# Mixture-of-experts stage: units of two tiles in place of single tiles, with gathered rows transposed first

## The reference, cut to what matters

```python
def reference(x, ...):                      # x: (2, 2048, 256) fp32
    xn = layernorm(x)
    # attention part: a scan over time whose weights depend on time_decay and time_first alone
    k, v = xn @ key_w.T, xn @ value_w.T
    r = sigmoid(xn @ recep_w.T)
    att = (r * wkv_scan(time_decay, time_first, k, v)) @ out_w.T
    # per step: p=max(pp,tf+pp); e1=exp(pp-p); e2=exp(tf+pp-p); wkv=(e1*aa+e2*v)/(e1*bb+e2+1e-6)
    #           p2=max(pp,td+pp); aa=exp(pp-p2)*aa+exp(td+pp-p2)*v; bb=exp(pp-p2)*bb+exp(td+pp-p2)
    # mixture of 8 experts, two per token, and one shared expert
    scores = softmax(xn @ gate_w.T + gate_b); top_w, top_i = top_k(scores, 2)
    y = sum over the two experts e of top_w * ((silu(xn@w1e.T+b1e) * (xn@w3e.T+b3e)) @ w2e.T + b2e)
    z = (silu(xn@ws1.T+bs1) * (xn@ws3.T+bs3)) @ ws2.T + bs2
    return x + att + y + z
```

## Time and profile before

| | |
|---|---|
| median of three runs | 540.8 us (540.36 to 542.17) |
| the profiled execution, its run | 540.79 us |
| its span | 539.1 us |
| mean granted clock of TensorE | 0.946 |
| PE busy | 471.3 us, 87% |
| PEld busy | 381.2 us, 71% |
| DVE busy | 428.3 us, 79% |
| ACT busy | 239.9 us, 44% |
| POOL busy | 260.9 us, 48% |

### The profile page before, as it was taken

How to read it: one execution, slowest core, us unless ns; L and a number is a source line. 1 busy time by engine, 2 the same in 40 slices (tenths; PEclk the granted TensorE clock), 3 DMA queues, 4 the chain that set the end, 5 groups by cost and what they waited for, 6 DMA issues and landing times. The chain is left out here.

```text
span 539.1 us, 10721 instructions
## 1 busy us (share of the span) xinstructions
PE 471.3 (87%) x2624; PEld 381.2 (71%) x2625; DVE 428.3 (79%) x963; ACT 239.9 (44%) x543; POOL 260.9 (48%) x311
## 2 busy tenths in 40 slices
PE   1885094999899999999999868899999999999997
PEld 1332042787788878777877757687889888888887
DVE  7797993578878888888888835998978888797964
ACT  1677251366556656565655555314232324242321
POOL 2000003535656666666566546787656573747200
PEclk9998555899989999999999997999999999999999
DMA  7999201383333334333433327527171625254011
GB/s 246 387 362 319 96 0 29 107 276 113 125 101 113 107 116 127 108 118 115 125 109 108 109 76 230 189 89 233 43 212 57 198 82 171 84 170 131 26 39 41
DMA packets 58553, 73.95 MB, mean 137 GB/s; under 512 B 6848, under 2 KB 47552, under 8 KB 58528
## 3 DMA queue, kind: packets, MB, share of 16 engines
q1 hardware_dynamic: 52048, 55.94, 31.0%
q0 software_dynamic: 6480, 17.70, 12.2%
HBM read 45.39 MB, written 28.18 MB: 136 GB/s over the span
## 5 line engine op out<-in xcount | busy, mean ns | idle before, releaser
L834 POOL DMA_INDIRECT xg<-xn_rows,picked x71 | 71.2, 1003 | 56.0 <-POOL picked L831 38.7
L1319 POOL DMA_INDIRECT yg<-expert_rows,rows x64 | 71.4, 1115 | 23.6 <-issue 17.1
L898 PE MATMUL ps_g<-w_hi,x_hi 128*128 x142 | 57.5, 405 | 0.8 <-issue 0.8
L898 PE MATMUL ps_g<-w_lo,x_hi 128*128 x142 | 56.9, 401 | 0.0
L898 PE MATMUL ps_g<-w_hi,x_lo 128*128 x142 | 56.9, 401 | 0.0
L831 POOL COPY picked<-tile_tok 128x1 int32 (+1 forms) x71 | 14.3, 201 | 86.5 <-POOLq L317 82.5
L1350 PE MATMUL ps_w<-col_hi,s_hi 128*128 128x512 f32 x128 | 51.0, 399 | 1.6 <-DVE res L1545 1.0
L971 ACT ACTIVATE act<-ps_g 128x256 f32<-128x256 f32 x71 | 27.2, 383 | 52.0 <-PE ps_g L901 48.4
L1351 PE MATMUL ps_w<-col_lo,s_hi 128*128 128x512 f32 x128 | 50.2, 392 | 0.0
L1352 PE MATMUL ps_w<-col_hi,s_lo 128*128 128x512 f32 x128 | 50.2, 392 | 0.0
L1452 ACT ACTIVATE sact<-ps_w,vec_b 128x512 f32<-128x512 f32 x32 | 22.0, 687 | 59.6 <-PE ps_w L1352 47.6
(11 more groups left out here) (192 smaller groups left out, 1412.2 us busy)
## 6 DMA issues: line engine op xcount, KB each, us to landing
expert_rows<-y SPq DMA_DIRECT2D x71, 128.0 KB
table<-mix_tables SPq DMA_DIRECT2D x16, 384.0 KB, 5.2
xin<-x SPq DMA_DIRECT2D x16, 256.0 KB, 4.2
xn_rows<-xn SPq DMA_DIRECT2D x16, 256.0 KB, 4.7
xn_columns<-xT SPq DMA_DIRECT2D x8, 512.0 KB, 4.5
col<-xn_columns SPq DMA_DIRECT2D x8, 512.0 KB, 7.3
mix_tables<-coef SPq DMA_DIRECT2D x16, 256.0 KB
res<-x SPq DMA_DIRECT2D x16, 256.0 KB
```

The costliest lines, as they stand in the source:

```text
L834: pool.indirect_dma_start(out=xg[a.buf(NG)][:], out_offset=None, in_=xn_d[:, :], in_offset=bass.IndirectOffsetOnAxis(ap=picked[a.buf(NG)][ ...
L898: nc.tensor.matmul(out, x[:, k, :], w[:, ds(e, 1), k, cols].rearrange("p o n -> p (o n)"), start=(k == 0 and n == 0), stop=False)
L1319: pool.indirect_dma_start(out=yg[a.buf(2)][:, k, q, :], out_offset=None, in_=y_d[:, :], in_offset=bass.IndirectOffsetOnAxis(ap=picked[a.bu ...
```

## The change

The expert stage works in units of two tiles (DUOS = 36, the last one with a single tile), and all its loops are written out. Each operation of ScalarE and VectorE on a tile becomes one on two tiles (128x512 in place of 128x256), each store one of 256 KB. A gather copies two columns of indices at once and issues two indirect DMAs, each with a semaphore step ahead; `xg` has four buffers of two tiles, and TensorE waits for both. `ps_x`, `ps_h`, `act1` and `hid` have one buffer of two tiles in place of two of one tile. TensorE's order for unit a is: read the two expert numbers of unit a+2, turn_x(a+3), turn_h(a), down(a-1), up(a+2). So the gathered rows are transposed first and the gated rows second. VectorE's order is gate(a+1), hidden(a+1), cut_h(a), cut_x(a+3), with hidden directly behind gate.

The table task works in pieces of 256 time steps (PIECE = 256, 8 pieces), a piece per four units, that is eight tiles. Its buffers are shared: `dif` lies in raw_vr, one of the two `firsts` in col0, the halves are written to `firsts` and `decay` themselves, the reciprocal overwrites `den`, and coef overwrites `firsts`. The loads of raw_vr and col0 move to the end of the stage. The first piece's growth, sums and halves stand ahead of the first tile's x_hi and x_lo. In the mix a table is one transfer.

```diff
-ROUNDS = -(-TILES // 4)
-REST = TILES - 4 * (ROUNDS - 1)
+DUOS = -(-TILES // 2)
-PIECE = 128
+PIECE = 256
...
-        picked = [sb(f"picked{b}", [P, 1], I32) for b in range(NG)]
-        xg = [sb(f"xg{b}", [P, C], F32) for b in range(NG)]
-        x_hi = [sb(f"x_hi{b}", [P, KC, P], F32R) for b in range(2)]
-        x_lo = [sb(f"x_lo{b}", [P, KC, P], F32R) for b in range(2)]
-        act1 = [sb(f"act1{b}", [P, FF], F32) for b in range(2)]
-        hid = [sb(f"hid{b}", [P, FF], F32) for b in range(2)]
-        h_hi = [sb(f"h_hi{b}", [P, KC, P], F32R) for b in range(2)]
-        h_lo = [sb(f"h_lo{b}", [P, KC, P], F32R) for b in range(2)]
+        picked = [sb(f"picked{b}", [P, 2], I32) for b in range(NG)]
+        xg = [sb(f"xg{b}", [P, 2, C], F32) for b in range(NG)]
+        x_hi = [sb(f"x_hi{b}", [P, 2, KC, P], F32R) for b in range(2)]
+        x_lo = [sb(f"x_lo{b}", [P, 2, KC, P], F32R) for b in range(2)]
+        act1 = sb("act1", [P, 2, FF], F32)
+        hid = sb("hid", [P, 2, FF], F32)
+        h_hi = [sb(f"h_hi{b}", [P, 2, KC, P], F32R) for b in range(2)]
+        h_lo = [sb(f"h_lo{b}", [P, 2, KC, P], F32R) for b in range(2)]
...
-        rden = sb("rden", [P, KC, PIECE], F32)
-        coef = sb("coef", [P, 2, KC, PIECE], F32)
-        ps_x = [bank(f"ps_x{b}", [P, KC, P]) for b in range(2)]
-        ps_g = [bank(f"ps_g{b}", [P, 2 * FF]) for b in range(2)]
-        ps_h = [bank(f"ps_h{b}", [P, KC, P]) for b in range(2)]
-        ps_y = [bank(f"ps_y{b}", [P, C]) for b in range(2)]
+        ps_x = bank("ps_x", [P, 2, KC, P])
+        ps_g = [bank(f"ps_g{b}", [P, 2, 2 * FF]) for b in range(2)]
+        ps_h = bank("ps_h", [P, 2, KC, P])
+        ps_y = [bank(f"ps_y{b}", [P, 2, C]) for b in range(2)]
...
+                def store_decay(v):
+                    sp.wait_ge(t_exp, v + 1)
+                    sp.dma_start(tab_d[v:v + 1, :, 0:1].rearrange("o p n k t -> p (o n k t)"),
+                                 decay[:].rearrange("p k t -> p (k t)")).then_inc(t_est, 16)
+
+                def store_coef(v):
+                    sp.wait_ge(t_coef, v + 1)
+                    sp.dma_start(tab_d[v:v + 1, :, 1:3].rearrange("o p n k t -> p (o n k t)"),
+                                 firsts[v % 2].rearrange("p n k t -> p (n k t)")).then_inc(t_cst, 16)
+
+                for a in range(DUOS + 1):
+                    if a > 0:
+                        store(a - 1)
+                    v, r = divmod(a, 4)
+                    if r == 1 and v < NPIECE:
+                        store_decay(v)
+                    if r == 2 and 0 < v <= NPIECE:
+                        store_coef(v - 1)
+                    if 0 < a <= len(loads):
+                        sp.dma_start(*loads[a - 1]).then_inc(c_ld, 16)
+                    if a == 4 * LAST_V + 1:
+                        sp.wait_ge(t_sides, NPIECE)
+                        sp.dma_start(raw_vr[:], wvr).then_inc(c_vr, 16)
+                    if a == 4 * LAST_V + 3:
+                        assert (LAST_V - 1) % 2 == 0
+                        sp.wait_ge(t_cst, LAST_V * 16)
+                        sp.dma_start(col0[:].rearrange("p k n -> p (k n)"), columns).then_inc(c_col, 16)
...
                 def gather(a):
+                    b, n = a % NG, tiles(a)
+                    at_least(pool, c_tx, a - NG + 1)
+                    nc.gpsimd.tensor_copy(picked[b][:, 0:n], tile_tok[:, 2 * a:2 * a + n]).then_inc(c_idx, 1)
+                    pool.wait_ge(c_idx, a + 1)
+                    for t in range(n):
+                        pool.sem_inc(c_go, 1)
+                        pool.indirect_dma_start(
+                            out=xg[b][:, t, :], out_offset=None, in_=xn_d[:, :],
+                            in_offset=bass.IndirectOffsetOnAxis(ap=picked[b][:, t:t + 1], axis=0)
+                        ).then_inc(c_gath[b], 16)
+
+                def denominator(v):
+                    own = OwnIn(pool, t_pool, At(0, v, NPIECE), 2)
+                    f = firsts[v % 2]
+                    pool.wait_ge(t_bb, v + 1)
+                    pool.wait_ge(t_exp_f, v + 1)
+                    at_least(pool, t_coef, v)
+                    own.link(nc.gpsimd.tensor_tensor(den[:], f[:, 0], s_b[:, :, 0:PIECE], ALU.mult))
+                    own.link(nc.gpsimd.tensor_tensor(den[:], den[:], f[:, 1], ALU.add))
                     own.close()
                     nc.gpsimd.tensor_scalar(den[:], den[:], 1e-6, 2.0, ALU.add, ALU.mult).then_inc(t_den, 1)
 
+                def factors(v):
+                    f = firsts[v % 2]
+                    pool.wait_ge(t_rec, v + 1)
+                    nc.gpsimd.tensor_tensor(f, f, den[:, None].broadcast_to([P, 2, KC, PIECE]),
                                             ALU.mult).then_inc(t_coef, 1)
 
+                for a in range(NG):
+                    gather(a)
+                for a in range(DUOS):
+                    v, r = divmod(a, 4)
+                    if a + NG < DUOS:
+                        gather(a + NG)
+                    if r == 1 and 0 < v <= NPIECE:
+                        factors(v - 1)
+                    if r == 2 and v < NPIECE:
+                        denominator(v)
+                for n, (raw, hi, lo) in enumerate((vr, col)):
                     pool.wait_ge(c_whi, n + 1)
                     nc.gpsimd.tensor_tensor(lo[:], raw[:], hi[:].bitcast(F32), ALU.subtract).then_inc(c_wlo, 1)
 
             @block.tensor
             def _(pe):
+                def experts(a):
+                    _, values = nc.values_load_multi_w_load_instructions(
+                        tile_exp[0:1, 2 * a:2 * a + tiles(a)], engines=[mybir.EngineType.PE],
+                        min_val=0, max_val=E - 1)
+                    return values
+
                 def turn_x(a):
+                    pe.wait_ge(c_gath[a % NG], a // NG * 32 + tiles(a) * 16)
+                    at_least(pe, c_xlo, a)
+                    for t in range(tiles(a)):
+                        for k in range(KC):
+                            mm = nc.tensor.transpose(ps_x[:, t, k, :], xg[a % NG][:, t, k * P:(k + 1) * P], ident[:])
                     mm.then_inc(c_tx, 1)
...
+                def down(a, es):
+                    pe.wait_ge(c_hlo, a + 1)
+                    at_least(pe, c_yc, a - 1)
+                    for t in range(tiles(a)):
+                        mm = three(ps_y[a % 2][:, t, :], h_hi[a % 2][:, t], h_lo[a % 2][:, t], es[t],
+                                   slice(2 * FF, WALL))
+                    mm.then_inc(c_y, 1)
+
+                es = {}
+                turn_x(0)
+                turn_x(1)
+                es[0] = experts(0)
+                up(0, es[0])
+                turn_x(2)
+                es[1] = experts(1)
+                up(1, es[1])
+                for a in range(DUOS):
+                    if a + 2 < DUOS:
+                        es[a + 2] = experts(a + 2)
+                    if a + 3 < DUOS:
+                        turn_x(a + 3)
+                    turn_h(a)
+                    if a > 0:
+                        down(a - 1, es.pop(a - 1))
+                    if a + 2 < DUOS:
+                        up(a + 2, es[a + 2])
+                down(DUOS - 1, es.pop(DUOS - 1))
...
+                def halves(v):
+                    f = firsts[v % 2]
+                    act.wait_ge(t_dif, v + 1)
+                    at_least(act, t_cst, (v - 1) * 16)
+                    at_least(act, t_est, v * 16)
+                    at_least(act, t_bb, v)
+                    nc.scalar.activation(f[:, 1], dif[:, 0], ACT.Relu, scale=-1.0)
+                    nc.scalar.activation(f[:, 0], dif[:, 0], ACT.Relu)
+                    nc.scalar.activation(decay[:], dif[:, 1], ACT.Relu).then_inc(t_sides, 1)
+
+                def exps(v):
+                    f = firsts[v % 2]
+                    act.wait_ge(t_sides, v + 1)
+                    nc.scalar.activation(decay[:], decay[:], ACT.Exp, scale=-1.0).then_inc(t_exp, 1)
+                    if v == 0:
+                        act.wait_ge(t_feed, 2)
+                    for c in range(KC):
+                        nc.scalar.activation(f[:, 0, c, :], f[:, 0, c, :], ACT.Exp, scale=-1.0, bias=feed[:, c:c + 1])
+                    nc.scalar.activation(f[:, 1], f[:, 1], ACT.Exp, scale=-1.0).then_inc(t_exp_f, 1)
+
+                halves(0)
+                cut_x(0)
+                cut_x(1)
+                silu(0)
+                cut_x(2)
+                for a in range(DUOS):
+                    v, r = divmod(a, 4)
+                    silu(a + 1)
                     cut_h(a)
+                    cut_x(a + 3)
+                    if a > 0:
+                        result(a - 1)
+                    if r == 0 and v < NPIECE:
+                        exps(v)
+                    if r == 3 and v < LAST_V:
+                        halves(v + 1)
+                    if a == DUOS - 3:
+                        act.wait_ge(c_vr, 16)
```

(55 more changed lines are left out.)

369 lines of the change are left out of this document (95 added, 274 removed).

## The result

| kernel | median us (lowest to highest) | profiled span us |
|---|---|---|
| before | 540.6 (539.8 to 542.2) | 539.1 |
| changed | 550.6 (545.4 to 550.8) | 549.0 |

The changed kernel takes 1.0158 times as long as the one before (95% interval 1.0094 to 1.0223). The forecast was 536.2 us, range 526.5 to 544.0: the sign was wrong, and the time lies outside the range. The interval leaves 1 out, so the change costs time, some 1 to 2%. Of the changed kernel's four executions three took 550.5 to 550.8 and one 545.4; their mean granted clock was 0.937 to 0.938 and 0.947, and 0.009 of 549 us is 4.9 us. That would be the whole distance if all of it fell while TensorE had work, which isn't shown: there is no trace of the shorter one. The profiled one is of the longer three.

The account below looks back on a forecast made before the run. It took a ring through GpSimd and VectorE to set the pace, TensorE 18.4 us idle or slow. 18.4 - 11.5 (late gathers, end) - 2.8 (start) = 4.1, plus 0.5 from the mix: 540.8 - 4.6 = 536.2 us, range 526.5 to 544.

Parts of the forecast that it names:

- term for late gathers: Expert stage: TensorE waits for gathered rows 1.7 us in each of six rounds, 0.5 for a lone tile: 10.7 us idle.
- GpSimd's low parts: End of the expert stage: two operations of 2.4 us each end about as the last store lands; cost nothing, barrier stays.
- Rival 1: TensorE's clock falls to half in the rounds, 1.7 us each; six falls give 546.4; chance of one or more 0.17.
- the rule against the change: TensorE: transposes don't count as busy for the clock like matmuls, so new pauses count longer; all rounds could bring a fall.
- single table transfer: Mix: tables come in one transfer and not two of 512-byte pieces; gain 0.5 us, bounds 0 and 1.
- The 0.8 us for the last unit's down-projection: End of the expert stage: the last down-projection waits for ScalarE, which has a 1.07 us copy in front; cost 0.8 us.
- the ring: Kernel before, expert stage: reciprocals, coef, gathers and denominator through GpSimd and VectorE take 12.68 us per four tiles; TensorE needs 11.6.
- The start: First up-projection stands behind the fourth descriptor instruction, not the second: 2.5 us later, some 0.3 more at half clock.
- single buffers: act1, hid, ps_x, ps_h: cost nothing while VectorE's side work stays under 3.1 us per unit; bound 0 to 3 us.
- the path: GpSimd's queue from last reciprocal over coef, gather, denominator to second gather: rows ready at s+19.0, wanted at s+17.3.
- rival 2: GpSimd's queue: descriptor gap 0.79 in each pair and not 0.30, 1.0 us more per round, 542.2 us; chance 0.13.
- Rival 3: The new path through GpSimd doesn't reach TensorE, only its own work is left: 525.5 us; chance 0.2.

Follow-up runs that it names:

- lows_dve: Changed kernel with the low parts vr_lo and col_lo at the expert stage's end moved from GpSimd to VectorE: 545.5 us, ratio 1.0103.
- before_lows: Kernel before with the low parts vr_lo and col_lo moved from GpSimd to VectorE in its last turn: 536.6 us, ratio 0.9939.
- rec_early: Changed kernel with VectorE's last reciprocal of a piece moved one unit earlier (4v+1 to 4v): 531.1 us, ratio to before 0.9834.
- mix_hold: Changed kernel with GpSimd waiting for VectorE's part_a before adding the bias in the mix's first step: 547.0 us, ratio 1.0141.
- store_late: Changed kernel with SyncE storing the coefficients (512 KB) one unit later: 558.7 us, ratio 1.0343.
- before_den_early: Kernel before with GpSimd's denominator put ahead of the last of a turn's gathers: 536.7 us, ratio 0.9934.
- two_tables: Changed kernel with each table of the mix loaded in two transfers of 512-byte pieces, as before: 544.9 us, ratio 1.0083.
- best: Changed kernel with the edits of rec_early, lows_dve and mix_hold at once: 521.1 us, ratio to before 0.9617.
- best_early: Kernel best with the first up-projection put ahead of the second unit's transposes: 521.7 us, ratio 0.9655.
- coef_first: Changed kernel with SyncE sending the coefficients ahead of the unit's results and not behind them: 547.7 us, ratio 1.0139.

## Why the prediction was wrong, point by point

Forecast -4.6, found +9.9 in the profiled execution: 14.5 us, in five steps. The largest lies in the sum's term for late gathers, "6 x 1.7 + 0.5 = 10.7": it measured 14.9 + 3.3 = 18.2. With one stretch at half clock that is 19.9 us, more than the 18.4 that the change was to remove.

1. **GpSimd's low parts cost "nothing": 2.2 us.** I let col_lo end "about as the last store lands" and took the barrier as fixed. It isn't: it follows GpSimd, and col_lo moved from 318.86 to 325.64 because its turn came behind coefficients that wait for the last reciprocal (317.56), 4.7 us later than before (312.88 to 318.59), and take 2.4 us in place of 1.3. lows_dve and before_lows show it. The trace of the kernel before had the number, 6.2 us from GpSimd's last end to the mix, but I had only looked at the copy and the first DMA of the earlier trace rows.
2. **The rounds: 2.5 late and not 1.7, 4.7 us in six rounds** (the first, 2.4 without its clock, counted with them: 14.9 against 10.2). The mechanism was right, and the steps up to the second gather came within 0.4 us. The small copy ahead of each gather takes 0.58 and 0.46 beside VectorE's work in place of 0.2, the second gather's descriptors come 0.3 to 0.4 later than drawn, and the second gather's rows are turned 3.35 us after its last descriptors start (228.35 to 231.70), where I had 2.9 from an undisturbed one. What delays that landing wasn't separated.
3. **The last round: 3.3 and not 0.5, 2.8 us.** I priced a lone tile at the second gather; the late one is the first, a pair: 298.01 to 303.41, 5.4 us from descriptors to transposes. With the coefficients sent ahead of it the landing is 4.5 and the pause 2.15; what else holds it wasn't tested. rec_early removes it whole.
4. **The clock: 1.7 us.** One fall, at 148.3, behind the pause of 2.33; the kernel before has one at the same place (149.5), which the sum took as gone. Rival 1 gave a fall or more 0.17, on pauses of 1.1 at most; the pause was twice that. Behind the pauses of 1.4 to 1.5 with eight transposes following it never fell in this trace, and not behind the one of 3.08 either. In other traces it did fall behind longer ones, and not always: behind 3.27 in mix_hold, and behind three of five of 1.9 to 2.1 in store_late. So the rule against the change didn't come out in the five rounds with pauses of 1.4 to 1.5, and the chain of six falls was rightly thought unlikely.
5. **The mix: +3.1 and not -0.5, 3.6 us.** The single table transfer was looked at only for who waits for the table. What it moved was the next transfer in SyncE's queue, the rows of x: GpSimd no longer waited for them and started its two large operations beside part_a. mix_hold gives 3.6 us back with this wait alone.

The 0.8 us for the last unit's down-projection didn't appear: the stage without pauses measures 206.6 us in rec_early (0.2 from the floor of 206.4), so steps 2 to 4 make 9.2; with 0.2 for the floor and less 0.8 that is the 8.6 by which the stage missed, and with 2.2 and 3.6 the 14.4 of 14.5.

The reading that the change was built on was wrong too, without harm to the sum: "what sets the pace is a ring". before_den_early takes VectorE's waits of the ring away and gains 3.8 of the 18.4 us.

**What was right.** The start, though not to the tenth that the number shows: 0.5 of its 2.8 us is that the stage before ended later in this execution (GpSimd's first copy of the expert stage at 87.31 and not 86.85); from that copy to the first up-projection pass 10.2 to 10.5 us in the ten traces with this start and 8.1 to 8.3 in the three of the old form, so 2.0 to 2.4 belong to the change, against 2.5 + 0.3. Then the floor of 2.89 us a tile, reads of expert numbers at nothing, single buffers for act1, hid, ps_x and ps_h at nothing, the two late loads, the ring gone and the path in its place, descriptors 0.30 apart (rival 2 wrong). A part of VectorE's side work was outside its bound: reciprocal and scan took 4.6 us in one unit (215.21 to 219.80), above the 3.1 allowed. It cost nothing that the trace shows: VectorE was through with that unit's tile work at 222.30, and without a pause TensorE would have come for it at 223.4.

**The steps that failed** are thus two sizes in the term for late gathers (rounds, last round), the clock, the low parts and the barrier taken as fixed, and a path in the mix that wasn't looked for. Behind them is one habit: each row's duration was taken from a place where it ran alone or undisturbed, and the "nothing" of a step was checked against one neighbour. The range had no case for three places missing at once, each for 2 to 5 us.

**Rival 3** ("the path doesn't reach TensorE", 525.5) was wrong for this kernel, and nearest to what the form can do: without the path, rec_early runs at 531.1. In its trace the distance to the mix is 1.4 us longer than before (6.6 for 5.2) and the mix 3.5 longer than forecast (217.0 for 213.5), points 1 and 5; that is 4.9 of the 5.6 us.

## What to carry to other kernels

When a change makes an engine's steps fewer and larger, write the new queue of each engine out to the end, and ask of every step what runs on the other engine in that microsecond; two engines that were never busy together before may be now. Before a stage's end is called fixed, look which engine is last against the barrier. And where a path is some 15% too long (19.9 us to TensorE's 17.3), look for the one instruction on it that can be issued a unit earlier: here 0.94 us of reciprocal was worth 20 us.

## What the runs showed of the hardware

- **An operation of VectorE with two inputs in SBUF and one of GpSimd don't run side by side, and VectorE's can be passed over twice.** part_a is issued at 344.30, while a descriptor instruction of GpSimd runs (343.96 to 344.91), and GpSimd's two products follow without a gap (344.91, 347.26); part_a does its 1.2 us only behind both. Five more of the runs show it, with the product 0.06 to 0.51 us behind part_a (5.87 to 6.32 us). But where GpSimd had stood idle and its product came second, it was GpSimd that waited, as in the fourth step of the same trace, where the product takes 3.25 in place of 2.40:

```profile
417.45 1.23 DVE L1477 TENSOR_TENSOR part_a<-sa,table 128x1024 f32<-128x1024 f32 x1
417.69 3.25 POOL L1299 TENSOR_TENSOR col_lo<-col,col_hi 128x1024 fp32r<-128x1024 f32 x1 [7.97 <-ACT col_hi L1406]
```

  The kernel before has both too: 4.25 us for part_a at 359.40, issued between the start of one product and the next, and 1.23 at 407.44. A descriptor instruction alone doesn't hold part_a: in two_tables one ran from 344.27 to 345.21, and part_a took 1.22. The Trainium skill (SBUF — State Buffer, Who interferes with whom) says that an instruction of VectorE with two SBUF inputs contends with one of GpSimd that reads SBUF, that the lock is exclusive, and that the order of issue decides which of the two blocks. The trace agrees on the lock (6.41 against 1.22 us) and, at 417.45, on the order; at 344.30 it doesn't: part_a was issued 0.61 us ahead of the first product and came behind the second. The measurement decides; what made the difference stays open.
- **Others that were longer beside GpSimd:** the scan of s_b (3.59 for 1.43 us) and a copy of 128x2 (1.23 us at 222.22 beside the denominator's first product, 0.16 in rec_early). The tile work of 128x512 with one input in PSUM kept its 0.66 to 0.69 us throughout.
- **The mix begins 6.2 us after GpSimd's last elementwise operation or 0.9 after ScalarE's last copy, whichever is later.** In the eleven kernels here in which GpSimd was the later, both old and new form, the distance was 6.16 to 6.18; in the other three (before_lows, best, best_early) the mix began 0.9 behind the last copy's end. What takes the 6.2 us wasn't looked into.
- **In the five middle rounds the rows of a pair of gathers are turned 3.1 to 3.4 us after the start of its second descriptor instruction with 256 KB stored beside it, and 3.7 to 3.8 with 512 KB more** (coef_first against the changed kernel). In the first and the last round it is 4.5 to 5.4 us in both, for reasons that no run separates.
